# Per-token maxima: the running maxima copied over the minima under a mask from ScalarE, then one product, in place of two products and a max

## The reference, cut to what matters

```python
# x = x + attn_b(layernorm(x)): for each token, H=16 heads, C=64 channels per head
Q = (x @ Wq + bq).reshape(b, s, H, C) * inv_sqrt_c
K = (x @ Wk + bk).reshape(b, s, H, C)
V = (x @ Wv + bv).reshape(b, s, H, C)
scores = jnp.einsum('bshq,bshk->bshqk', Q, K)          # an outer product: q_i * k_j
mask = jnp.triu(jnp.ones((C, C), dtype=bool), 1)
scores = jnp.where(mask, -jnp.inf, scores)             # k_j counts only for j <= i
w = jax.nn.softmax(scores, axis=-1)
attn = jnp.einsum('bshqk,bshk->bshq', w, V).reshape(b, s, HID)
return attn @ Wo + bo
```

## Time and profile before

| | us |
|---|---|
| median of three runs | 2081.5 |
| the profiled execution's own time | 2084.54 |
| its span, first to last instruction | 2082.5 |
| what lies around the span | 2.04 |

### The profile page before, as it was taken

How to read it: one execution, slowest core, us unless ns; L and a number is a source line. 1 busy time by engine, 2 the same in 40 slices (tenths; PEclk the granted TensorE clock), 3 DMA queues, 4 the chain that set the end, 5 groups by cost and what they waited for, 6 DMA issues and landing times. The chain is left out here.

```text
span 2082.5 us, 35441 instructions
## 1 busy us (share of the span) xinstructions
PE 1836.3 (88%) x14080; PEld 1359.7 (65%) x14080; DVE 1875.1 (90%) x1681; ACT 1120.8 (54%) x1469; POOL 1395.1 (67%) x655
## 2 busy tenths in 40 slices
PE   3899999999856989889898998988989989899886
PEld 2344444444243777769777787877877878778785
DVE  7887887887266999999999999999999999999994
ACT  3376777676612455455554555555455554555552
POOL 5122222222201989989889898898988989989890
PEclk8899999999965999999999999999999999999996
DMA  3300000000000000000000000000000000000000
GB/s 105 65 6 8 9 7 8 9 5 1 1 1 0 1 1 1 1 1 1 1 1 2 1 1 2 1 1 2 1 1 1 2 1 1 2 1 1 1 1 20
DMA packets 11094, 14.28 MB, mean 7 GB/s; under 512 B 4672, under 2 KB 7776, under 8 KB 10816
## 3 DMA queue, kind: packets, MB, share of 16 engines
q1 hardware_dynamic: 9216, 8.91, 2.0%
q10 hardware_dynamic: 1728, 3.12, 0.4%
HBM read 4.65 MB, written 1.05 MB: 3 GB/s over the span
## 5 line engine op out<-in xcount | busy, mean ns | idle before, releaser
L1065 POOL TENSOR_TENSOR b_p_ring<-b_p_ring,b_m 128x2048 f32<-128x2048 f32 (+7 forms) x384 | 1249.5, 3300 | 198.8 <-DVE b_p_ring L979 196.8
L1101 ACT ACTIVATE b_p_ring<-b_p_ring 128x2048 f32<-128x2048 f32 (+7 forms) x384 | 532.8, 1412 | 640.7 <-POOL b_p_ring L1065 640.0
L1167 PE MATMUL b_ps<-k_ident,b_ev_ring 128*128 128x128 f32 (+6 forms) x4608 | 581.0, 276 | 100.8 <-DVE b_ev_ring L1025 100.7
L1025 DVE TENSOR_TENSOR b_ev_ring<-b_p_ring,b_ps 128x2048 f32<-128x2048 f32 (+7 forms) x384 | 636.9, 1663 | 1.5 <-ACT b_p_ring L1101 1.3
L979 DVE TENSOR_TENSOR b_p_ring<-b_ps,b_key 128x2048 f32<-128x2048 f32 (+7 forms) x384 | 636.8, 1666 | 0.0
L1167 PE MATMUL b_ps<-k_ident,b_p_ring 128*128 128x128 f32 (+6 forms) x4608 | 578.6, 276 | 33.3 <-issue 22.2
L1167 PEld LDWEIGHTS b_ps<-k_ident,b_ev_ring 128*128 128x128 f32 (+6 forms) x4608 | 496.3, 136 | 155.5 <-DVE b_ev_ring L1025 131.4
L1167 PEld LDWEIGHTS b_ps<-k_ident,b_p_ring 128*128 128x128 f32 (+6 forms) x4608 | 512.9, 137 | 41.6 <-issue 25.1
L589 DVE TENSOR_REDUCE a_negm<-a_ps 128x1 f32<-128x768 f32 (+7 forms) x384 | 354.9, 955 | 90.0 <-PE a_ps L478 88.6
L572 ACT ACTIVATE a_ex<-a_ps 128x512 f32<-128x512 f32 (+3 forms) x768 | 334.2, 498 | 176.6 <-PE a_ps L517 174.9
L408 POOL TENSOR_SCALAR_AFFINE_SELECT a_ex<-a_ex 128x512 f32<-128x512 f32 x128 | 81.2, 635 | 365.1 <-ACT a_ex L572 365.0
(11 more groups left out here) (174 smaller groups left out, 981.1 us busy)
## 6 DMA issues: line engine op xcount, KB each, us to landing
rk_of_group<-rows_k SPq DMA_DIRECT2D x96, 32.0 KB, 1.9
rq<-rows_q SPq DMA_DIRECT2D x42, 64.0 KB, 2.4
k_wqkv<-in_wqkv ACTq DMA_DIRECT2D x1, 2048.0 KB, 10.3
out<-x_all SPq DMA_DIRECT2D x4, 256.0 KB, 2.3
k_wo<-in_wo ACTq DMA_DIRECT2D x1, 512.0 KB, 10.3
rq<-rows_q SPq DMA_DIRECT2D x12, 32.0 KB, 2.0
k_w_attn<-in_w_attn ACTq DMA_DIRECT2D x1, 192.0 KB, 3.1
k_reset_min<-in_reset_min ACTq DMA_DIRECT2D x1, 128.0 KB, 10.4
```

The costliest lines, as they stand in the source:

```text
L1025: nc.vector.tensor_tensor(chunk(ev_ring, c), chunk(p_ring, c), over_queries(values(c), c), ALU.mult).then_inc(ev_done.sem, 1)
L1065: nc.gpsimd.tensor_tensor(pc, pc, over_rows(m[:, half].rearrange("p i h -> p (i h)"), c), ALU.subtract).then_inc(shifted.sem, 1)
L1101: nc.scalar.activation(pc, pc, ACT.Exp).then_inc(exp_done.sem, 1)
L1167: last = nc.tensor.matmul(ps[0:width, bank, b // IB * P:(b // IB + 1) * P], rows[:, r, b:hi].rearrange("p i h -> p (i h)"), k["ident"][:], ...
```

## The change

The max over two products is replaced by a choice. ScalarE writes max(q, 0) of the half's queries into the free bank. VectorE copies the running maxima over the running minima wherever that value's bits are not zero, that is where q is positive, and then takes one product of q with what now stands in kminr. ScalarE's step has its place after the exponential of chunk 13 for half 1, and after that of chunk 21 for half 0 of the next tile, which is behind invert and turn_back of chunk 20. For the first tile it stands behind the first turn_back. VectorE waits for it on a new semaphore, and counts up another one (sign_seen) that nothing waits for.

```diff
@@ phase_b
     HJ_AT, SCAN_AT, TURN_BACK_AT = (14, 16), (15, 17), 20
+    SIGN1_AT, SIGN0_AT = 13, 21
     Q1_AT, Q0_AT, V1_AT, V0_AT = 11, 19, 16, 23
...
-        m_step = sem("m_step", 6)
+        rising = sem("rising", 2)
+        sign_seen = sem("sign_seen", 2)
+        m_step = sem("m_step", 4)
...
             def maxima(it, half):
                 q = ps[:, Q_BANK].rearrange("p (i h) -> p i h", h=H)
-                t = ps[:, ACC_BANK + 2 * half + 1].rearrange("p (i h) -> p i h", h=H)
                 at = lambda r: r[:, half * FIRST:(half + 1) * FIRST, :]
                 dve.wait_ge(q_psum.sem, q_psum.at(it, half + 1))
                 dve.wait_ge(turned_back.sem, turned_back.at(it, 2))
-                nc.vector.tensor_tensor(m[:, half], q, at(kmaxr), ALU.mult).then_inc(m_step.sem, 1)
-                nc.vector.tensor_tensor(t, q, at(kminr), ALU.mult).then_inc(m_step.sem, 1)
-                dve.wait_ge(m_step.sem, m_step.at(it, 3 * half + 2))
-                nc.vector.tensor_tensor(m[:, half], t, m[:, half], ALU.max).then_inc(m_step.sem, 1)
+                dve.wait_ge(rising.sem, rising.at(it, half + 1))
+                dve.sem_inc(sign_seen.sem, 1)
+                positive = ps[:, ACC_BANK + 2 * half + 1].rearrange("p (i h) -> p i h", h=H)
+                nc.vector.copy_predicated(at(kminr), positive.bitcast(mybir.dt.uint32), at(kmaxr)).then_inc(m_step.sem, 1)
+                dve.wait_ge(m_step.sem, m_step.at(it, 2 * half + 1))
+                nc.vector.tensor_tensor(m[:, half], q, at(kminr), ALU.mult).then_inc(m_step.sem, 1)
...
-                    pool.wait_ge(m_step.sem, m_step.at(it, 3 * half + 3))
+                    pool.wait_ge(m_step.sem, m_step.at(it, 2 * half + 2))
...
+            def take_sign(it, half):
+
+                act.wait_ge(q_psum.sem, q_psum.at(it, half + 1))
+                nc.scalar.activation(ps[:, ACC_BANK + 2 * half + 1], ps[:, Q_BANK], ACT.Relu).then_inc(rising.sem, 1)
...
                     if c == INVERT0_AT:
                         invert(it, 0)
+                    if c == SIGN1_AT:
+                        take_sign(it, 1)
+                    if not last and c == SIGN0_AT:
+                        take_sign(it + 1, 0)
                     if not last and c == TURN_BACK_AT:
                         turn_back(it + 1)
...
             turn_back(0)
+            act.wait_ge(key_taken.sem, 2)
+            take_sign(0, 0)
             all_tiles(act, tile)
```

## The result

The kernel is slower: a median of 2104.1 us against 2082.15 us of the kernel before on the same chip, ratio 1.0105 with a 95% interval of [1.0091, 1.0119], so +22 us. (One execution of 6428.6 us is left out of both figures.) The profiled execution took 2104.59 us with a span of 2102.9, against 2084.54 and 2082.5: +20.4 us of span, which is what the traces have to explain. The forecast was +12, that is 2093.5 us, with a range of 2088 to 2099 for its own case and of 2085 to 2109 with the cheap and the dear masked copy taken in.

A forecast was written before the change was run, and what follows sets the result against it. VectorE's work (85.32 us a tile) and a loop through shift 20 and turn_back (85.38) bound the kernel together. 15 x 0.70 + 16 x 0.11 = 12.3, taken as 12, gave 2093.5 us; range 2088 to 2099, with rival copies 2085 to 2109.

The forecast's parts named there:

- its own case: The forecast with a masked copy of 0.69 us: 2093.5 us, range 2088 to 2099.
- dear masked copy: Rival: masked copy takes 1.22 us like a scan, 17 us on top of 12, 2110.5 us; chance 0.09.
- Two chains: At half 0's maxima, VectorE's own work and the chain exponential 20, invert, turn_back arrive 0.06 us apart.
- the loop through shift 20: One tile: half 0 maxima, VectorE's work to multiply 20, shift 20, exponential 20, invert, turn_back, maxima again; 85.38 us.
- the gap before shift 20: Sign: GpSimd's idle time ahead of shift 20 stays 0.6 to 0.7 us; closed would mean half 1's delay was absorbed.
- Half 0, 0.70 per tile: Next tile's half 0: max(q, 0) behind turn_back and exponential 21 makes chunk 0's multiply 0.70 us later.
- Half 1, 0.11 per tile: Half 1: max(q, 0) follows the queries, so the 0.60 us saved goes on the wait; chunk 16's multiply 0.11 later.
- The queries' time is tied to VectorE's: Half 1: TensorE adds chunk 10's value product when VectorE ends it, so queries won't come earlier relative to VectorE.
- The first tile and the end: First tile: ScalarE's 0.60 us meets the 0.60 saved, so nothing; 2 us either way allowed for the first tiles.
- VectorE alone sets the pace: Rival: new waits are covered and each of 32 halves gives 0.60 us, -19 us, 2062.5; chance 0.09.
- the table loads: Rival: max(q, 0) needs another table, a 1283 ns load ahead of it in both halves, 2133.5 us; chance 0.03.
- the cheap copy: Rival: masked copy takes 0.43 us, both delays shrink by 0.26, 4.5 us in all, 2086; chance 0.10.

The follow-up runs named there:

- The square of four kernels: Kernel before; changed kernel 1.0105; changed kernel without max(q, 0) and its wait 0.9945; kernel before with max(q, 0) and the wait added, unused, 1.0162.
- The kernel with TensorE kept busy: Changed kernel with three unused products on TensorE, two ahead of adding up chunk 21's value product, one after chunk 23: 1.0089, median 2100.9 us.
- with both waits covered: Changed kernel with turn_back split by halves, max(q, 0) of half 0 earlier and TensorE's queries of both halves earlier: 0.9923, median 2065.0 us.
- the moves' own: Kernel before with its two products and a max, turn_back split by halves and queries of both halves earlier: 0.9991, median 2079.0 us.
- the kernel with the wait alone: Kernel before, old three instructions kept, with ScalarE's max(q, 0) and VectorE's wait for it added, unused: 1.0162, median 2118.2 us.
- with the halves: Changed kernel, half 1's queries ahead of the keys, turn_back split: half 0's copies, max(q, 0), then half 1's copies; 0.996, median 2074.0 us.

## Why the prediction was right, and where its sizes were off

The mechanism holds step by step. Two chains met 0.06 us apart at the maxima of half 0; the change shortened VectorE's and lengthened ScalarE's, and the loop through shift 20 passed it on to the tile. The masked copy starts 1.49 us after the second copy has ended (1.41 by the forecast's times), the period rose, the waits moved to the new step, GpSimd's idle time before its first shift rose to 5.58 (5.4 forecast), and the gap before shift 20 has not closed (0.99; 0.6 to 0.7 forecast). The square of four kernels shows both parts by themselves: the wait +33.5 us, the instructions -11.7.

The forecast of +12 is 10 us short of the median, 8 short of the profile's +20; 2104 lies above the 2088 to 2099 of the forecast's own case. That it lies under 2109 is luck: that end of the range was there for a dear copy, which did not come (and it was drawn a little too low, since the dear case by its own sum gives 2110.5). By its terms:

- *Half 0, 0.70 per tile: measured 0.84.* The copy takes 0.753 instead of 0.69 us, so the dependent product starts after 0.78 instead of 0.73. The handover from max(q, 0) took 0.25, where 0.11 and, for the count, 0.05 were added; what the further queue instruction costs was mis-sized. max(q, 0) itself was 0.58 for 0.60. Over fifteen tiles 12.0 instead of 10.5: 1.5 us.
- *Half 1, 0.11 per tile: measured 0.36 and 0.24.* The same two terms, 0.06 and 0.09, and in even tiles 0.11 more in the handover (1585.94 - 1585.57 = 0.37). 4.3 instead of 1.8 us over sixteen places: 2.5 us. The sixteenth place was read wrongly: the last tile has no keys to form, its queries come early, and it wins 0.55 us instead of losing 0.11. This was the poorest estimate in proportion, since it was a small difference between two large terms (0.60 saved, 0.71 spent), and an error of 0.1 in either doubles it.
- *"The queries' time is tied to VectorE's": true only while TensorE keeps up.* The step failed in four of sixteen tiles. It was read from one place with TensorE on time, 0.06 us behind the earlier trace rows, though the trace of before has it late in tiles 3, 5 and 7. After the longer spell at the lower clock it was 0.5 to 1.0 us behind, and the product L1029 waited too. 1.8 + 1.0 us were left out. The kernel with TensorE kept busy shows where they come from.
- *The first tile and the end,* taken as nothing, made 0.7 us.

Together 1.5 + 2.5 + 2.8 + 0.7 = 7.5 of the 8 us between the forecast and the two traces. VectorE's busy time fell by 16.6 us instead of 22, of which the copy's extra length, 32 x 0.06, explains 2; busy time counts overlaps once, so this sum was too coarse.

Of the rivals, the one in which VectorE alone sets the pace is not what the change did, but what it could have done: with both waits covered it came out at 2065.0, against 2062.5 worked out for it, 1.9 us of the gain being the moves' own. The rule of the Trainium skill behind that rival (VectorE: DVE Perf Modes, Rules for kernel authors: keep down the count of chained operations) thus holds for this pair once nobody else is waited for. The kernel with the wait and without the copy shows what it leaves out: one more wait costs 33.7 us with the count of VectorE's operations unchanged. The dear copy (1.22 us) and the table loads are refuted by 753 ns and by loads at two lines alone; the cheap copy (0.43) as well.

What stays open: the extra 0.11 us of the handover at half 1 of even tiles, which the kernel with the wait alone has too, and why the idle time at the loop's turn leaves a longer spell at 1.2 GHz after the change (6.8 us) than before it (3.6), though the idle times are alike.

## What to carry to other kernels

Where an engine is busy 85.31 of 85.38 us, look at once for the chain that arrives with it: saving its instructions by a step on another engine trades work for a wait, and the wait's place decides the sign. The same pair of instructions was worth +22 us with the new step where the change put it, and -16 us with its inputs taken earlier, 2 of them the moves' own. So before giving the idea up, ask which order on the helping engines makes the new operand early, and follow the wait: here it went from ScalarE's order to the size of its copies and then to TensorE's order, and each took one small move.

## What the runs showed of the hardware

- A masked copy of 512 f32 elements, mask in PSUM, source and destination in SBUF, took 753 ns (725 to 772 over 32), and the product that needs its result started 0.78 us after its start; a product of that size takes 690 ns with 0.73 to a dependent one. It did not slow GpSimd's shifts beside it: those of 2048 elements took 4577 ns in the mean of 150, before 4576.
- From the end of an activation to the start of a VectorE instruction that waits for it: 0.14 us when the queue instruction that waits for it is the last one ahead (wait alone; and with the halves, where it carries a count as well), 0.25 with one more queue instruction behind it, 0.34 with two. At half 1 of even tiles the first two were 0.24 and 0.37.
- TensorE's idle time at the turn of the two-tile loop, 0.8 to 1.0 and then 2.4 to 2.5 us in tile 11 (2.1 to 2.8 for the longer part in tiles 3 to 13) without anything waited for that the profile shows, was followed by matmuls at 1.2 GHz (16 in 3.24 us instead of 1.91). With three unused products in and around that place the granted clock stayed at 1.00 from 745 to 2050 us, and the kernel was no slower for the added work.
